# A two-layer attention kernel: the second layer's first and last steps in written-out orders, and one product moved in the first layer's third turn

## The reference, cut to what matters

```python
# layer 0
xn = layer_norm(x, norm_w, norm_b)
q, k, v = xn @ q_w + q_b, xn @ k_w + k_b, (xn @ v_w + v_b) * mask
att = softmax(einsum('bnhl,bmhl->bnmh', q, k) + (1 - mask) * -1e6, axis=2)
y = einsum('bnmh,bmhl->bnhl', att, v)
h = layer_norm(y, sb_norm_w, sb_norm_b) * (1 + scale) + shift
x = x + silu(h) @ out_w + out_b
# layer 1
xn = layernorm(x)
q, k, v = xn @ Wq + bq, where(mask, -inf, xn @ Wk + bk), where(mask, 0, xn @ Wv + bv)
attn = einsum('bhse,bhsd->bhed', softmax(k, axis=rows), v)
y = einsum('bhtd,bhed->bhte', softmax(q, axis=head columns), attn)
h = layernorm(y) * (1 + scale) + shift
out = x + silu(h) @ film_out_W + film_out_b
```

## Time and profile before

| | |
|---|---|
| median of 3 runs | 918.88 us |
| the profiled execution | 921.37 us |
| its span, first to last instruction | 919.3 us |
| mean granted TensorE clock | 0.985 of full |
| busy: PE, DVE, ACT, POOL | 95%, 83%, 73%, 67% |
| turns of the first layer | 0 to about 542 us |
| rounds of the second layer | about 542 us to the end |

### The profile page before, as it was taken

One profiled execution on the slowest core, in us unless ns is written; L12 is line 12 of the kernel. 1 busy time (PEld: TensorE's weight loads), 2 busy tenths in 40 slices (PEclk: granted clock), 3 DMA queues, 4 the chain that ended last, 5 costly groups with the idle time before them and its releaser, 6 DMA issues.

```text
span 919.3 us, 23736 instructions
## 1 busy us (share of the span) xinstructions
PE 873.9 (95%) x8432; PEld 727.9 (79%) x8432; DVE 763.3 (83%) x1569; ACT 670.3 (73%) x1200; POOL 616.8 (67%) x1096
## 2 busy tenths in 40 slices
PE   5889999999999999999999879999999999999994
PEld 4677777777777777777776558899999999999984
DVE  5658999999999999999998566788888888888873
ACT  2237777777777767677777866888888888888873
POOL 3434757575757575756564355888888888888873
PEclk9869999999999999999999999999999999999999
DMA  8734353434344444343433312133222222222111
GB/s 266 236 111 166 113 177 121 169 129 161 137 155 142 148 145 150 140 155 137 156 124 133 120 63 75 39 89 95 93 83 82 82 82 81 82 81 82 35 41 46
DMA packets 77396, 108.54 MB, mean 118 GB/s; under 512 B 7072, under 2 KB 43392, under 8 KB 77152
## 3 DMA queue, kind: packets, MB, share of 16 engines
q1 hardware_dynamic: 77280, 107.03, 34.8%
HBM read 35.60 MB, written 16.88 MB: 57 GB/s over the span
## 4 chain that ended last, share of the span: by engine, by line
PE 55%; POOL 30%; issue 8%; DVE 3%; ACT 2%; DMA 1%; SPq 1%; POOLq 0%; ACTq 0%; DVEq 0%
PE psX L1142 16%; PE psY L1257 13%; POOL sb_rs L462 6%; PE psT L1238 6%; PE psT L1219 5%; POOL sb_v L498 4%; POOL sb_u L453 4%; POOL sb_w L493 4%; POOL sb_v L470 4%; PE psY L1278 3%; PE psM L1238 3%; POOL sb_v L486 3%; PE psM L1219 2%; PE psX L1290 2%; POOL sb_ve L460 2%
## 5 line engine op out<-in xcount | busy, mean ns | idle before, releaser
L880 DVE TENSOR_REDUCE sb_cm<-psT 128x4 f32<-128x1024 f32 x168 | 202.6, 1216 | 20.8 <-PE psT L1238 20.6
L562 ACT ACTIVATE sb_P<-psT 128x1024 f32<-128x1024 f32 x176 | 178.0, 1028 | 29.8 <-PE psT L1219 14.7
L1257 PE MATMUL psY<-sb_P,sb_Vp 128*17 128x256 f32 x2048 | 129.2, 381 | 0.6 <-DVE sb_yr L906 0.4
L880 DVE TENSOR_REDUCE sb_cm<-psM 128x4 f32<-128x1024 f32 x88 | 107.0, 1216 | 7.7 <-PE psM L1238 7.6
L1142 PE MATMUL psX<-sb_xT,sb_W0h 128*128 128x256 f32 x488 | 96.4, 301 | 2.0 <-DVE sb_xT L886 2.0
L400 POOL TENSOR_SCALAR sb_ve<-sb_mv 128x2 f32<-128x2 f32 x32 | 7.3, 228 | 135.6 <-DVE sb_mv L914 135.6
L562 ACT ACTIVATE sb_P<-psM 128x1024 f32<-128x1024 f32 x80 | 82.1, 1026 | 14.5 <-PE psM L1219 6.7
L1257 PEld LDWEIGHTS psY<-sb_P,sb_Vp 128*17 128x17 f32 x2048 | 50.5, 97 | 46.3 <-issue 5.5
L417 POOL TENSOR_TENSOR sb_qp<-sb_qp 128x512 fp32r<-128x512 f32 x64 | 81.9, 1280 | 5.3
L1238 PE MATMUL psT<-sb_Ks,sb_Qs 64*128 64x256 f32 x672 | 75.6, 308 | 3.9 <-DVE sb_cm L880 1.9
L1142 PEld LDWEIGHTS psX<-sb_xT,sb_W0h 128*128 128x128 f32 x488 | 74.2, 199 | 6.3 <-DVE sb_xT L886 2.4
(11 more groups left out here) (180 smaller groups left out, 2577.5 us busy)
## 6 DMA issues: line engine op xcount, KB each, us to landing
sb_Qs<-sb_qp SPq DMA_DIRECT2D x96, 256.0 KB
sb_Ks<-sb_qp SPq DMA_DIRECT2D x96, 256.0 KB
sb_xt<-in_x SPq DMA_DIRECT2D x32, 256.0 KB, 3.1
y_normed<-sb_Yn SPq DMA_DIRECT2D x32, 256.0 KB, 2.0
sb_u<-in_x SPq DMA_DIRECT2D x32, 256.0 KB, 2.9
sb_u<-y_normed SPq DMA_DIRECT2D x32, 256.0 KB, 3.1
out<-sb_w SPq DMA_DIRECT2D x32, 256.0 KB, 2.2
sb_v<-key_mask SPq DMA_DIRECT2D x32, 128.0 KB, 3.5
```

The costliest lines, as they stand in the source:

```text
L562: a.activation(P[G % 4][:, :], pairs[place["S", n, g][0]][:, :], ACT.Exp).then_inc(s_ex, 1)
L880: v.tensor_reduce(cm[n % 2][:, 4 * j:4 * j + 4], scores, AX.X, ALU.max, negate=True).then_inc(s_mx, 1)
L1257: ins = pe.matmul(psY[32 * j:32 * j + 17, y0:y0 + T], Vp[n % RING][:, m, 4 * gr + j, :], Pj[:, c0:c0 + 256], start=(m == 0), stop=(m == 1))
```

## The change

Four edits, none of which adds or removes a computation. The helpers `late` and the argument of `freed` go; `second(t)` tests `ok` in place of `late` (those hunks are left out below).

- Each engine but SyncE runs `second(t)` only for t = 4 to 31. Ahead of it a list in an order of its own takes the place of rounds 2 and 3, behind it one that takes the place of rounds 32 to 37.
- PE's head is now `qv_(0)`, `tr_(1)`, `k_(0)`, `f0_(2)`, `qv_(1)`, `f0_(3)`, `k_(1)`, `o0_(2)`, `kt_(0)`, `kv_(0)`, `qt_(0)`, `qt_(1)`, `y_(0)`, `tr_(2)`. In its tail `y_(31)` stands ahead of `f1_(30)` and `o1_(28)`, and `kt_(30)` and `kt_(31)` ahead of `y_(29)` and `f1_(29)`.
- In turns 34 to 36 steps of batches 0 and 1 move: `o0_(0)` from the start of turn 35 to the end of turn 34, `tr_(0)` with `xT_(0)` and `xl_(0)` from turn 36 into turn 35, ahead of a `yturn` and a `divide`; `u_(1, 0)`, `t_(1, 0)`, `hh_(1, 0)` and `h_(1, 0)` by one to three places forward in turns 34 and 35; `xo_(0)` from turn 36 to turn 35.
- In turn 2 `qk(2, 1)` on PE moves ahead of `rowmax(2, 5)` and `rowmax(2, 6)`.

```diff
--- before.py
+++ after.py
@@ -42,11 +42,6 @@
 def landed(n, ring, copies=1):
 
     return 16 * copies * (n // ring + 1)
-
-
-def late(n):
-
-    return EARLY <= n < B
 
 
 def stage(t, i, lag):
@@ -237,11 +232,10 @@
 
         block = ctx.enter_context(nc.Block())
 
-        def freed(eng, t):
-
-            if t == EARLY:
-                eng.wait_ge(s_sT, 8 * B)
-                eng.wait_ge(s_pv, 4 * B)
+        def freed(eng):
+
+            eng.wait_ge(s_sT, 8 * B)
+            eng.wait_ge(s_pv, 4 * B)
 
         @block.sync
         def _(sp):
...
@@ -528,19 +521,46 @@
                     vmask(t - 1)
                 if ok(t + 1):
                     xnorm(t + 1)
+                if t == B + 1:
+                    xb_(0)
+                    xb_(1)
                 if ok(t):
                     split(t, 0)
                     split(t, 1)
-                if t == B + 1:
-                    xb_(0)
-                    xb_(1)
                 if t == B + 3:
                     rs_(1, 0, e_xn)
-                if t == B + 4:
                     xo_(0)
-                    xo_(1)
-            for t in range(EARLY, ROUNDS):
+            freed(g)
+            xo_(1)
+            xb_(2)
+            xb_(3)
+            kb_(0)
+            qs_(0)
+            ken_(0)
+            kb_(1)
+            qs_(1)
+            rs_(2, 0, e_xn)
+            ken_(1)
+            xo_(2)
+            rs_(0, 1, e_yn)
+            for t in range(4, B):
                 second(t)
+            kb_(B - 2)
+            rs_(B - 1, 0, e_xn)
+            ken_(B - 2)
+            qs_(B - 2)
+            hl_(B - 5)
+            kb_(B - 1)
+            rs_(B - 3, 1, e_yn)
+            ken_(B - 1)
+            qs_(B - 1)
+            hl_(B - 4)
+            rs_(B - 2, 1, e_yn)
+            hl_(B - 3)
+            rs_(B - 1, 1, e_yn)
+            hl_(B - 2)
+            hl_(B - 1)
+            xo_(B - 1)
 
         @block.scalar
         def _(a):
...
@@ -728,8 +747,6 @@
                     embedded(1)
                 if t == B + 2:
                     t_(0, 0)
-                if t == B + 3:
-                    hh_(1, 0)
                 exps(t, 0)
                 if ok(t - 4):
                     yturn(t - 4, 0)
@@ -748,8 +765,14 @@
                     a.activation(tc[:, :, :], psY[:, 0:4 * B].rearrange("p (k b) -> p k b", k=4), ACT.Tanh,
                                  scale=0.5).then_inc(p_act, 1)
                 exps(t, 4)
+                if t == B + 2:
+                    u_(1, 0, r_f0)
                 if ok(t - 4):
                     yturn(t - 4, 1)
+                if t == B + 2:
+                    t_(1, 0)
+                if t == B + 3:
+                    xT_(0)
                 if ok(t - 2):
                     cturned(t - 2)
                 if t == 0:
@@ -757,24 +780,66 @@
                 exps(t, 5)
                 if t == B + 1:
                     u_(0, 0, r_f0)
-                if t == B + 2:
-                    u_(1, 0, r_f0)
                 if ok(t):
                     qk(t, 1)
                 exps(t, 6)
                 if t == B + 2:
-                    t_(1, 0)
+                    hh_(1, 0)
                 exps(t, 7)
-                if t == B + 4:
-                    xT_(0)
-                    xn_(1)
-                    xT_(1)
                 if t == 1:
                     embedded(0)
                 if t == 2:
                     gathered()
-            for t in range(EARLY, ROUNDS):
+            freed(a)
+            xn_(1)
+            xT_(1)
+            vk_(0)
+            u_(2, 0, r_f0)
+            t_(2, 0)
+            hh_(2, 0)
+            ke_(0)
+            vk_(1)
+            u_(3, 0, r_f0)
+            t_(3, 0)
+            kn_(0)
+            ke_(1)
+            qe_(0)
+            hh_(3, 0)
+            xn_(2)
+            xT_(2)
+            for t in range(4, B):
                 second(t)
+            hh_(B - 6, 1)
+            qe_(B - 3)
+            t_(B - 5, 1)
+            kn_(B - 3)
+            yn_(B - 4)
+            ke_(B - 2)
+            xn_(B - 1)
+            vk_(B - 2)
+            xT_(B - 1)
+            u_(B - 4, 1, r_f1)
+            hh_(B - 5, 1)
+            qe_(B - 2)
+            kn_(B - 2)
+            t_(B - 4, 1)
+            ke_(B - 1)
+            vk_(B - 1)
+            yn_(B - 3)
+            hh_(B - 4, 1)
+            kn_(B - 1)
+            u_(B - 3, 1, r_f1)
+            t_(B - 3, 1)
+            qe_(B - 1)
+            yn_(B - 2)
+            hh_(B - 3, 1)
+            u_(B - 2, 1, r_f1)
+            t_(B - 2, 1)
+            hh_(B - 2, 1)
+            yn_(B - 1)
+            u_(B - 1, 1, r_f1)
+            t_(B - 1, 1)
+            hh_(B - 1, 1)
 
         @block.vector
         def _(v):
...
@@ -1084,7 +1148,6 @@
                     v.wait_ge(p_pe, 9)
                     v.tensor_tensor(rb[:, 2, :], rb[:, 2, :], psT[0][:, 512:768], ALU.add).then_inc(p_ve, 1)
                 if t == B + 3:
-                    h_(1, 0)
                     x1_(0)
                     hl_(1)
                     st0_(0)
@@ -1104,9 +1167,6 @@
                 if t == B + 3:
                     x1_(1)
                     st0_(1)
-                if t == B + 4:
-                    xl_(0)
-                    xl_(1)
                 maxima(t, 3)
                 if t >= 4:
                     for_later(t - 4)
@@ -1117,8 +1177,12 @@
                 maxima(t, 4)
                 if t >= 1 and ok(t + 1):
                     stats(t + 1, 1)
+                if t == B + 2:
+                    h_(1, 0)
                 maxima(t, 5)
                 maxima(t, 6)
+                if t == B + 3:
+                    xl_(0)
                 if ok(t - 4):
                     divide(t - 4, 0)
                 maxima(t, 7)
@@ -1128,8 +1192,59 @@
                     vbias(t)
                 if ok(t - 4):
                     divide(t - 4, 1)
-            for t in range(EARLY, ROUNDS):
+            freed(v)
+            dq_(0)
+            xl_(1)
+            mq_(0)
+            dk_(0)
+            h_(2, 0)
+            dq_(1)
+            hl_(2)
+            kd_(0)
+            mq_(1)
+            dk_(1)
+            x1_(2)
+            st0_(2)
+            h_(3, 0)
+            bd_(0)
+            hl_(3)
+            kd_(1)
+            yd_(0)
+            xl_(2)
+            for t in range(4, B):
                 second(t)
+            st1_(B - 4)
+            x1_(B - 1)
+            dk_(B - 2)
+            st0_(B - 1)
+            dq_(B - 2)
+            mq_(B - 2)
+            kd_(B - 2)
+            bd_(B - 3)
+            ob_(B - 6)
+            h_(B - 5, 1)
+            xl_(B - 1)
+            yd_(B - 3)
+            dk_(B - 1)
+            st1_(B - 3)
+            dq_(B - 1)
+            kd_(B - 1)
+            bd_(B - 2)
+            mq_(B - 1)
+            h_(B - 4, 1)
+            yd_(B - 2)
+            st1_(B - 2)
+            bd_(B - 1)
+            h_(B - 3, 1)
+            ob_(B - 5)
+            yd_(B - 1)
+            st1_(B - 1)
+            ob_(B - 4)
+            h_(B - 2, 1)
+            ob_(B - 3)
+            h_(B - 1, 1)
+            ob_(B - 2)
+            ob_(B - 1)
 
         @block.tensor
         def _(pe):
...
@@ -1494,8 +1608,6 @@
                     row(psT[0][:, 512:768], 1, 0).then_inc(p_pe, 1)
 
             for t in range(TURNS):
-                if t == B + 3:
-                    o0_(0)
                 rowmax(t, 0)
                 rowmax(t, 1)
                 scores(t, 0)
@@ -1513,9 +1625,6 @@
                 scores(t, 2)
                 if t == B + 3:
                     o0_(1)
-                if t == B + 4:
-                    tr_(0)
-                    tr_(1)
                 if t == 0:
                     first_column()
                 if ok(t):
@@ -1532,6 +1641,8 @@
                 scores(t, 4)
                 if ok(t - 4):
                     values(t - 4, 3)
+                if t == 2:
+                    qk(t, 1)
                 rowmax(t, 5)
                 scores(t, 5)
                 rowmax(t, 6)
@@ -1539,12 +1650,16 @@
                     cturn(t - 2)
                 if t == B + 1:
                     f0_(0)
-                if ok(t):
+                if ok(t) and t != 2:
                     qk(t, 1)
                 if t == 0:
                     second_column()
                 if t == 2:
                     embeddings(3)
+                if t == B + 2:
+                    o0_(0)
+                if t == B + 3:
+                    tr_(0)
                 if ok(t - 4):
                     yturn(t - 4, 0)
                 rowmax(t, 7)
@@ -1558,8 +1673,50 @@
                     embeddings(0)
                 if t == 2:
                     embeddings(4)
-            for t in range(EARLY, ROUNDS):
+            freed(pe)
+            qv_(0)
+            tr_(1)
+            k_(0)
+            f0_(2)
+            qv_(1)
+            f0_(3)
+            k_(1)
+            o0_(2)
```

(48 more changed lines are left out.)

## The result

Four runs of the changed kernel gave 902.54, 904.53, 905.15 and 906.84 us, median **904.8**; four of the kernel before, beside them, had a median of 918.75. The ratio is 0.985, 95% interval 0.982 to 0.988. The forecast was 908.1, range 902.5 to 913.6. The profiled execution is that of 906.84 us: span 904.7, 14.6 less than before.

The account below looks back on a forecast made before the run. TensorE, busy 95% of the span, was taken as the bound, so order could only win back its stops and slow stretches. 1.07 + 4.6 + 5.1 = 10.8 us off gave a median of 908.1 us, range 902.5 to 913.6.

Parts of the forecast that it names:

- rival 4: In turn 2 the clock stays high once PE's stop is shorter: 5 us more gained, 903 us; chance 0.08.
- the two signs of being wrong: A full round longer than 11.1 us, or PE's stops after `o0_(31)` still over 10 us ahead of `o1_(31)`.
- The third turn, forecast 1.07, unchanged clock: Turn 2: `qk(2, 1)` starts at 39.80, PE starts at 39.80 in place of 40.87; 1.07 us saved, clock as before.
- The end of the first layer, 0.25 late: Turns 34 to 36: the moved steps make `values(31, 0)` start at 531.8, net 0.25 us late; bounds 0 and 1.5.
- The head, 4.6: Start of the second layer: most PE stops go, `f0_(4)` comes at 560.0 in place of 564.55, 4.6 us earlier.
- The clock's 1.6: Between `tr_(0)` and `f0_(4)` before: the clock falls at 551, costing about 1.6 of the 23.31 us.
- 0.94 for `kn_(0)`: New order at the second layer's start: PE still stops 0.94 us for `kn_(0)` ahead of `kv_(0)`.
- 0.85 for `qe_(0)`: New order at the second layer's start: PE still stops 0.85 us for `qe_(0)` ahead of `qt_(1)`.
- the collision's 0.8: `h_(2, 0)`, `hl_(2)`, `h_(3, 0)` on VectorE lie beside GpSimd steps, `hl_(2)` holds up `o0_(2)`: 0.8 us, bounds 0 and 2.4.
- rival 3: Rounds 6 to 31: a stop of 0.77 us repeats in each of 26 full rounds, 20.0 us, so 928.1; chance 0.05.
- The tail, 5.1: Round 32 to the end: fewer PE stops and earlier `y_(31)`, end at 914.2 in place of 919.3; 5.1 us saved.
- The 1.2 us for a slow `o1_(31)`: At the end, a stop of 2.9 us ahead of `o1_(31)` brings half clock, so 1.2 us added.

Follow-up runs that it names:

- the two fills: Kernel before with 20 unread matmuls in PE's stop ahead of `rowmax(2, 5)`, 917.97 us (0.9986); or with `qk(2, 1)` done in both places, 916.51 us (0.9982).
- Experiment 5: Kernel after with two output buffers and GpSimd's `xb_(3)` behind `qs_(1)`: 903.88 us; the same with four unread products ahead of `o1_(31)`: 903.58 us.

## Why the prediction held, and where it did not

**The time.** 908.1 forecast, 904.8 measured, inside the range and within rival 4's 903 by 2 us. The forecast's own sum was 10.8 us; at equal clock the kernel is about 8.6 faster, at its own clock 14. Trace against trace it is 14.6, and the third turn's clock, 3.6, makes up nearly all that the sum lacks. So the terms held better than the total: that the median came out 3.3 us off and not more is in part luck, since it rests on how often the clock fell in the runs taken. Of the two signs of being wrong neither came: a full round took 11.06 us, and PE's stops from `o0_(31)` to `o1_(31)` sum to 6.6.

**The third turn, forecast 1.07, unchanged clock.** From `rowmax(2, 3)` to `values(30, 0)` it gave 482.00 - 476.86 = 5.1 us, of which 1.55 is order and 3.6 clock. The step that failed is "nothing of what PE did before 38.9 changes, so I take the clock as it was". The low stretch was no property of the kernel before but of about half of its runs, and one trace couldn't show that. The term was mis-sized too: 1.55 in place of 1.07, since `qk(2, 1)` started at 39.33 and not at 39.80; the eviction that it waits for ended at 38.79 in after, 39.75 in before. Rival 4 had the right place and a fair size; its reason, less standing still, is borne out by how often a very low mean clock appears, not by the means of the two fills.

**The end of the first layer, 0.25 late.** 0.42 in the trace of after, within its bounds.

**The head, 4.6.** `f0_(4)` came 27.8 us behind `values(31, 0)` in place of 33.0, 5.2 less: 4.6 + 0.25 had been forecast for that distance. The clock's 1.6 was right for that trace. Of the terms, 0.94 for `kn_(0)` was 0.69, 0.85 for `qe_(0)` was 0.78, and the collision's 0.8 was 0.59 at `o0_(2)`. Of the three steps that could collide two did; `h_(3, 0)` took 0.67 us, with only a small GpSimd step beside it, and that one took 0.58 in place of 0.22. Experiment 5 shows that this last term was no price of its own: without it another step is late by as much.

**Rounds 6 to 31** stayed at 11.06 us with PE full, so rival 3 falls; rounds 4 and 5 kept a stop of 0.68 us each.

**The tail, 5.1.** 5.11 in the trace, but two errors cancelled. `y_(31)` came 23.02 us after round 32 began, forecast 22.6, with stops of 0.96 and 0.73 for the forecast 1.0 and 0.85, so the order was right. The 1.2 us for a slow `o1_(31)` did not come. In its place the output buffer's chain took about 1 us. The sentence "by the pass `o1_(30)` ends at 905.0, well before `hl_(31)`" failed: it rested on a DMA of 2.3 us, and one took 4.05. `o1_(30)` ended at 897.9, only 0.8 us ahead of `hl_(31)`, and `ob_(30)`, which `o1_(31)` also waits for, came at 898.39 behind the next DMA. It was missed too that `ob_(28)` stands behind `st1_(31)` in VectorE's queue, so that `y_(31)` sets when the buffer's chain starts.

## What to carry to other kernels

Read the granted clock of several runs before you cost a low stretch of one trace: here it was worth some 5 us beside 8.6 for the orders, and it came and went with nothing changed. Follow a single output buffer through the last batches with its longest DMA, not its usual one. And ask what the removal of one short stop among several will bring up: here it brought up the next, 0.81 us for 0.59.
